# A fused gated-attention and quantised-MLP kernel: the first three steps of its software pipeline written out by themselves

## What is computed

```python
v    = ctx @ Wkv[:, 1024:]
x    = x + tanh(g_xattn) * (v @ Wout + bout)
h    = layernorm(x) * ln1_g + ln1_b          # over 256
h    = bitlinear(h, w1, b1)                  # 256 -> 1024
h    = gelu(h)
h    = layernorm(h) * ln2_g + ln2_b          # over 1024
h    = bitlinear(h, w2, b2)                  # 1024 -> 256
out  = x + tanh(g_ffn) * h
# bitlinear: each row of the input rounded to 127 steps of its largest
# magnitude, the weights to -1, 0, 1 of their mean magnitude
```

## Time and profile before

| | |
|---|---|
| three runs | 412.28, 412.6 and 414.04 us, median 412.6 |
| the profiled execution | 411.33 us, its span 409.5 us |
| busy in the span | DVE 327.3 us (80%), PE 309.5 (76%), ACT 277.6 (68%), POOL 221.4 (54%) |
| mean granted clock of PE | 0.946 |

### The profile page before, as it was taken

How to read it: one execution, slowest core, us unless ns; L and a number is a source line. 1 busy time by engine, 2 the same in 40 slices (tenths; PEclk the granted TensorE clock), 3 DMA queues, 4 the chain that set the end, 5 groups by cost and what they waited for, 6 DMA issues and landing times.

```text
span 409.5 us, 5758 instructions
## 1 busy us (share of the span) xinstructions
PE 309.5 (76%) x1658; PEld 186.5 (46%) x1658; DVE 327.3 (80%) x794; ACT 277.6 (68%) x446; POOL 221.4 (54%) x117
## 2 busy tenths in 40 slices
PE   2846777687969697979797969797979684938365
PEld 2744643343636363636363636363636341515043
DVE  0345461998999999999999999999999996968681
ACT  1202237598887878787888888787878776969421
POOL 4000416577566666666666666666666666664600
PEclk9988889998999999999999999999999996969688
DMA  7941223316365555556555555555552526353625
GB/s 225 378 149 47 81 91 108 89 51 115 117 116 169 113 170 112 171 104 182 108 175 107 178 105 179 103 179 104 128 101 81 101 79 88 93 96 86 153 53 154
DMA packets 98557, 51.59 MB, mean 126 GB/s; under 512 B 87407, under 2 KB 89640, under 8 KB 98526
## 3 DMA queue, kind: packets, MB, share of 16 engines
q1 hardware_dynamic: 96608, 51.00, 49.1%
q10 hardware_dynamic: 1918, 0.23, 0.4%
HBM read 21.78 MB, written 8.46 MB: 74 GB/s over the span
## 4 chain that ended last, share of the span: by engine, by line
DVE 41%; PE 30%; issue 12%; POOL 7%; DMA 5%; ACT 3%; DVEq 0%; POOLq 0%; ACTq 0%
DVE y L657 10%; PE bank_f L904 8%; POOL rstd L295 6%; PE slot_c L864 5%; DVE h L616 5%; DVE amax L624 5%; DVE res L707 5%; PE slot_a L890 4%; DVE amax L661 3%; DMA split_vectors<-vec_parts 3%; PE slot_b L890 3%; DVE x L573 2%; DVE parts L559 2%; PE slot_a L887 2%; PE bank_q L794 2%
## 5 line engine op out<-in xcount | busy, mean ns | idle before, releaser
L311 POOL TENSOR_TENSOR y<-u,g_bc 128x1024 f32<-128x1024 f32 x64 | 150.2, 2369 | 28.7 <-DVE parts L559 25.4
L295 POOL TENSOR_TENSOR rstd<-var,half_neg 128x8 f32<-128x8 f32 x18 | 30.3, 1683 | 129.5 <-DVE var L698 86.1
L657 DVE TENSOR_TENSOR y<-y,slot_c 128x1024 f32<-128x1024 f32 x64 | 77.6, 1212 | 5.0 <-PE slot_c L864 5.0
L661 DVE TENSOR_REDUCE amax<-y 128x1 f32<-128x1024 f32 x64 | 78.1, 1220 | 2.2
L441 ACT ACTIVATE junk<-u,usum 128x1024 bf16<-128x1024 f32 x64 | 73.7, 1151 | 1.2
L414 ACT ACTIVATE q<-y,s 128x1024 f16<-128x1024 f32 x64 | 69.8, 1139 | 5.2 <-DVE s L688 5.0
L843 PE MATMUL bank_q<-wvo,ctxT 128*128 128x256 f32 x256 | 69.1, 402 | 0.0
L904 PE MATMUL bank_f<-w2T,q2T 128*128 128x256 f16 x512 | 64.1, 281 | 0.0
L904 PEld LDWEIGHTS bank_f<-w2T,q2T 128*128 128x128 f16 x512 | 51.5, 101 | 14.3 <-issue 0.8
L405 ACT ACTIVATE q<-h,s 128x256 f16<-128x256 f32 x64 | 27.3, 496 | 41.2 <-DVE s L648 41.1
L864 PE MATMUL slot_c<-ln_rows,rows 128*128 128x512 bf16 x128 | 40.9, 402 | 16.9 <-DVE y L657 8.5
(11 more groups left out here) (104 smaller groups left out, 393.1 us busy)
## 6 DMA issues: line engine op xcount, KB each, us to landing
c_in<-in_ctx SPq DMA_DIRECT2D x16, 512.0 KB, 3.3
x_in<-in_x SPq DMA_DIRECT2D x16, 512.0 KB, 4.6
out<-res SPq DMA_DIRECT2D x32, 256.0 KB, 2.4
y<-in_L_ffn_w SPq DMA_DIRECT2D x2, 1024.0 KB, 12.1
u<-in_L_xattn_Wkv SPq DMA_DIRECT2D x1, 1024.0 KB, 7.0
u<-in_L_xattn_Wout SPq DMA_DIRECT2D x1, 1024.0 KB, 10.6
q2T<-q SPq DMA_TRANSPOSE x64, 3.3
g_bc<-in_L_ffn_ln_g SPq DMA_DIRECT2D x1, 512.0 KB, 12.4
```

The source lines that it names most:

```text
L295: nc.gpsimd.tensor_tensor(rstd[:, :, :], var[:, :, :], half_neg[:, :, :], ALU.pow) \
L311: nc.gpsimd.tensor_tensor(y[:, k % 2, t, :], u[:, t, :], g2_bc[:, :], ALU.mult).then_inc(gain2_done, 1)
L657: nc.vector.tensor_tensor(line, line, slot_c[:, :], ALU.add).then_inc(y_done, 1)
L661: nc.vector.tensor_reduce(amax2[:, t:t + 1], y[:, k % 2, t, :], AX.X, ALU.max, apply_absolute_value=True).then_inc(amax2_done, 1)
```

## The change

- The split vectors go to memory in one transfer instead of three. `load_rows` and the load of `bout_rows` move from ACT to SP, which now waits for that transfer before it issues them and everything behind them (x of step 0, w2, the gains, the inputs of step 1). `load_rows` reads one copy of the three parts three times.
- Bodies -3, -2 and -1 are written out by themselves on PE, ACT and DVE; on POOL body(-2) makes the gain product of step 0 in two halves, ahead of the first root.
- `attention_bank` gives half 1 of step 0 the second half of `slot_c` and half 1 of step 1 `bank_f`, so these two do not wait for the residual of half 0.
- The turned context of step 2 is taken by ACT in body(0), behind `quantise_first(0)`; before, it was taken in body(-1).
- In `second_product` the bias comes behind the products of each group (two products of 256 columns) instead of ahead of both groups (one of 512 columns); the wait for `rows` moves with it.
- In the last body ACT rounds all four groups of step 15 and then takes the rows.

```diff
@@ -50 +50 @@
-    parts_dram = nc.dram_tensor("split_vectors", (NPROD, 4 * H), BF16, kind="Internal").ap()
+    parts_dram = nc.dram_tensor("split_vectors", (NPART, 4 * H), BF16, kind="Internal").ap()
@@ -183,0 +184,6 @@
+        def attention_bank(k, h):
+            if h == 1 and k < 2:
+                return slot_c[:, 512:1024] if k == 0 else bank_f[:, :]
+            return bank_q[:, :]
@@ -235,0 +242,13 @@
+            def load_rows(dst, first, kind, n):
+                source = parts_dram[:, first:first + n].unsqueeze(0).to_broadcast([NPART, NPART, n])
+                for a in range(2):
+                    at = ROWS * a + NPROD * kind
+                    col = n * a if dst.shape[1] > n else 0
+                    sp.dma_start(dst[at:at + NPROD, col:col + n], source).then_inc(rows_in, 16)
+            sp.wait_ge(parts_out, 16)
+            sp.wait_ge(rows_zero, 5)
+            sp.dma_start(bout_rows[0:NPART, :], parts_dram[0:NPART, 3 * H:3 * H + D]) \
+                .then_inc(bout_in, 16)
@@ -239,0 +259,2 @@
+            load_rows(ln1_rows[:, :], 3 * H + D, 0, D)
+            load_rows(ln1_rows[:, :], 3 * H + 2 * D, 1, D)
@@ -241,0 +263,4 @@
+            load_rows(b1_rows[:, :, :].rearrange("p a n -> p (a n)"), 0, 4, H)
+            load_rows(ln2_rows[:, :, :].rearrange("p a n -> p (a n)"), H, 2, H)
+            load_rows(ln2_rows[:, :, :].rearrange("p a n -> p (a n)"), 2 * H, 3, H)
+            load_rows(b2_rows[:, :], 3 * H + 3 * D, 5, D)
@@ -317 +342 @@
-                if i == -1:
+                if i == -2:
@@ -318,0 +344,7 @@
+                    for h in range(2):
+                        two = slice(2 * h, 2 * h + 2)
+                        pool.wait_ge(x1_done, h + 1)
+                        op = nc.gpsimd.tensor_tensor(
+                            h1[:, two, :], x1[:, 0, two, :],
+                            g1_bc[:, :].unsqueeze(1).to_broadcast([P, 2, D]), ALU.mult)
+                    op.then_inc(gain1_done, 1)
@@ -324 +356 @@
-                if live(i + 1):
+                if live(i + 1) and i > -1:
@@ -336,8 +367,0 @@
-            def load_rows(dst, first, kind, n):
-                v = dst.shape[1] // n
-                for a in range(2):
-                    at = ROWS * a + NPROD * kind
-                    act.dma_start(dst[at:at + NPROD, n * (a % v):n * (a % v) + n],
-                                  parts_dram[:, first:first + n]).then_inc(rows_in, 16)
@@ -361,4 +385,2 @@
-            for i in range(NPART):
-                act.dma_start(parts_dram[NPART * i:NPART * (i + 1), :]
-                              .rearrange("j (p n) -> j p n", p=P).rearrange("j p n -> p j n"),
-                              vec_parts[:, :, :]).then_inc(parts_out, 16)
+            act.dma_start(parts_dram[:, :].rearrange("j (p n) -> p j n", p=P), vec_parts[:, :, :]) \
+                .then_inc(parts_out, 16)
@@ -377,4 +398,0 @@
-            act.wait_ge(parts_out, 16 * NPART)
-            act.wait_ge(rows_zero, 5)
-            act.dma_start(bout_rows[0:NPART, :], parts_dram[0:NPART, 3 * H:3 * H + D]) \
-                .then_inc(bout_in, 16)
@@ -382,6 +399,0 @@
-            load_rows(ln1_rows[:, :], 3 * H + D, 0, D)
-            load_rows(ln1_rows[:, :], 3 * H + 2 * D, 1, D)
-            load_rows(b1_rows[:, :, :].rearrange("p a n -> p (a n)"), 0, 4, H)
-            load_rows(ln2_rows[:, :, :].rearrange("p a n -> p (a n)"), H, 2, H)
-            load_rows(ln2_rows[:, :, :].rearrange("p a n -> p (a n)"), 2 * H, 3, H)
-            load_rows(b2_rows[:, :], 3 * H + 3 * D, 5, D)
...
@@ -444,0 +458,2 @@
+                if i == -3:
+                    return
@@ -446 +461,11 @@
-                    weight_copies(0, [w1T[:, k, :] for k in range(KD)])
+                    take_context(1, 0)
+                    weight_copy(0, 0)
+                    take_context(1, 1)
+                    return
+                if i == -1:
+                    take_rows()
+                    weight_copy(0, 1)
+                    weight_copy(1, 0)
+                    weight_copy(1, 1)
+                    nc.scalar.activation(table[:, :], half_neg[:, 0, 0:1], ACT.Gelu)
+                    return
@@ -449,0 +475,3 @@
+                if i == 0:
+                    take_context(2, 0)
+                    take_context(2, 1)
@@ -453 +481 @@
-                if -1 <= i <= S + 1:
+                if i <= S:
@@ -458,4 +486,2 @@
-                if i == -1:
-                    weight_copies(1, [w2T[:, 4 * n:4 * n + 4, :].rearrange("p k d -> p (k d)")
-                                      for n in range(2)])
-                    nc.scalar.activation(table[:, :], half_neg[:, 0, 0:1], ACT.Gelu)
+                if i == S + 1:
+                    take_rows()
@@ -575 +601 @@
-                        in0=bank_q[:, :], scalar=tg[:, 0:1],
+                        in0=attention_bank(k, h), scalar=tg[:, 0:1],
@@ -718,0 +745,26 @@
+                    return
+                if i == -2:
+                    residual(0, 0)
+                    statistics(0, 0)
+                    residual(0, 1)
+                    statistics(0, 1)
+                    for n in range(4):
+                        join(0, n)
+                    scale_weights(1)
+                    round_weights(1, 0)
+                    return
+                if i == -1:
+                    deviations()
+                    for n in range(5):
+                        split(n)
+                    residual(1, 0)
+                    statistics(1, 0)
+                    round_weights(1, 1)
+                    shift_first(0)
+                    for n in range(5):
+                        first(0, n)
+                    residual(1, 1)
+                    statistics(1, 1)
+                    for n in range(4):
+                        join(1, n)
+                    return
@@ -724,4 +776 @@
-                if i == -2:
-                    scale_weights(1)
-                    round_weights(1, 0)
-                if -1 <= i <= S:
+                if i <= S:
@@ -729 +778 @@
-                if -1 <= i <= S + 1:
+                if i <= S + 1:
@@ -764,2 +812,0 @@
-                if i == -2:
-                    round_weights(1, 1)
...
@@ -836 +885 @@
-                    else:
+                    elif k > 1:
@@ -839 +888 @@
-                        acc = bank_q[:, (t % 2) * D:(t % 2 + 1) * D]
+                        acc = attention_bank(k, h)[:, (t % 2) * D:(t % 2 + 1) * D]
@@ -897 +945,0 @@
-                    wait(pe, rows_copied, k + 4)
@@ -899,2 +946,0 @@
-                    nc.tensor.matmul(bank_f[:, :], rows[:, pair, :], b2_rows[:, :], start=True,
-                                     stop=False)
@@ -901,0 +948 @@
+                        acc = bank_f[:, (t % 2) * D:(t % 2 + 1) * D]
@@ -904,4 +951,6 @@
-                            product = nc.tensor.matmul(bank_f[:, (t % 2) * D:(t % 2 + 1) * D],
-                                                       q2T[:, t, j, :], w2T[:, j, :], start=False,
-                                                       stop=(t % 2 == 1 and j == KH - 1))
-                        product.then_inc(ffn_done, 1)
+                            nc.tensor.matmul(acc, q2T[:, t, j, :], w2T[:, j, :], start=(j == 0),
+                                             stop=False)
+                        wait(pe, rows_copied, k + 4)
+                        nc.tensor.matmul(acc, rows[:, pair, :],
+                                         b2_rows[:, (t % 2) * D:(t % 2 + 1) * D], start=False,
+                                         stop=True).then_inc(ffn_done, 1)
@@ -910,2 +958,0 @@
-                    turn_weights(0, lambda n, j: w1_raw[:, j, n * P:(n + 1) * P])
-                    sum_weights(1)
@@ -914,2 +961,10 @@
-                if live(i + 2):
-                    attention(i + 2, 1)
+                    attention(0, 0)
+                    attention(0, 1)
+                    sum_weights(1)
+                    return
+                if i == -2:
+                    turn_context(1, 0)
+                    turn_weights(0, 0)
+                    turn_context(1, 1)
+                    attention(1, 0)
+                    return
@@ -916,0 +972,2 @@
+                    turn_rows()
+                    turn_weights(0, 1)
@@ -917,0 +975,11 @@
+                    shift_first(0)
+                    pe.wait_ge(wscaled, 2)
+                    attention(1, 1)
+                    turn_weights(1, 0)
+                    turn_weights(1, 1)
+                    turn_context(2, 0)
+                    turn_context(2, 1)
+                    attention(2, 0)
+                    return
+                if live(i + 2):
+                    attention(i + 2, 1)
@@ -950,4 +1017,0 @@
-                if i == -2:
-                    turn_weights(1, lambda n, j: w2_raw[:, j % KD, (4 * n + j // KD) * P:
-                                                        (4 * n + j // KD + 1) * P])
```

(27 more changed lines are left out.)

4 lines of the change are left out of this document (2 added, 2 removed).

## The result

The changed kernel takes **402.73 us** (median of 4 runs, 401.95 to 403.77), the kernel before, run beside it, 412.44 (4 runs, 411.33 to 414.04). The ratio is 0.977, 95% interval 0.9741 to 0.9798: faster by 2.3%, or 9.7 us. The forecast was 403.2.

What follows compares the result with a forecast made beforehand. Middle steps were taken as bound by DVE (19.32 of 20.56 us), the start as held by ACT's wait for the split vectors. 411.33 - 9.4 = 401.9 for a profiled-like execution, median 403.2, range 399.6 to 407.0.

Steps and rivals of the forecast that it cites:

- The copy of `wvo`, the landing: Start: `wvo` copied without waiting, 23.2 to 23.8 us; split vectors landed at 16, so nothing waits for loads.
- The rival's late landing: Start: split transfer lands at 20.2, w2 at 26.4, everything moves by 2.9 us to 406.1; chance 0.15.
- Attention of step 0: Start: each half takes 1.95 us at full clock, the second following at once; 25.75 and 27.7.
- Join and root: Start: residual, statistics and join take 2.70 us to POOL's root at 30.45; the root takes 2.48, to 32.95.
- Rows, then ACT's own queue: Start: rows copied at 35.15; then ACT's weight copies and GELU table, not DVE, set the rounding at 42.4.
- Copy, turn, copy: Start: after 1.71 us of rounding, ACT and PE handle the context of step 2 in 1.98, to 46.15.
- Attention of step 2: Start: PE, mostly idle before, runs mostly at the 1.2 GHz level and takes 3.44 us, to 49.6.
- Residual to rows: Start: residual of step 2 to copied rows takes 3.84 us, to 53.5; the transposing DMA is hidden.
- the middle keeps its length: Middle steps: no work is taken from DVE there, so steps stay at 20.56 us.
- The end and the biases: Second products and last body: worth nothing; bounds 0 to 0.80 us per step and 0 to 2.1 us gained.
- The rival of a broken stream: Every step: split biases break PE's stream, 0.80 us per step, 12.0 in all, giving 415.2; chance 0.05.
- 9.4 less: Start: first product of step 0 begins at 53.5 instead of 62.90 us, the whole predicted gain.

Runs made afterwards that it cites:

- loads_not_held: Changed kernel with SP issuing x of step 0, w2 and the first gain ahead of its wait for the split vectors: 402.42 us.
- steps_only: Changed kernel's order with the memory traffic of before (three transfers, wait and twelve row loads on ACT): 412.26 us, ratio 0.9997.
- transfers_only: Kernel before with the new memory part alone (one transfer, its wait and the row loads on SP), old order of bodies: 404.24 us, ratio 0.9806.
- old_end_and_bias: Changed kernel with the old 512-column bias ahead of both groups and the old order of rows and roundings at the end: 403.38 us.
- start_kept_busy: Changed kernel with 64 extra small PE products, 50 before Wv is there and 14 before the context of step 0: 403.09 us.
- one_transfer_act: Changed kernel with one transfer, but its wait and the row loads on ACT, nothing held on SP: 411.76 us, ratio 0.9983.
- pe_kept_busy: Changed kernel with 38 extra products in PE's pauses, around the turns of context 2 and ending bodies 0 and 1: 399.43 us.
- rounding_first: Changed kernel with ACT taking the context of step 2 before the rounding of step 0, w2 copies and GELU table load after it: 396.77 us.
- all_together: rounding_first with the transposing DMA of step 0 issued ahead of two loads, plus extra PE products at the start and ending bodies 0 and 1: 393.05 us.

## Why the prediction was right, and where it was off

The time (402.73 for 403.2) and the place (`hidden(0)` at 53.39 for 53.5) both came out. By its points:

1. *The copy of `wvo`, the landing.* Right: 22.74, the landing at about 16.0 for 16. The rival's late landing was then made on purpose in loads_not_held, and cost nothing, since there w2 and x were not behind it. So what a late landing does with w2 and x behind it was not measured. In the changed kernel the second sum did wait 0.48 us for w2, too little to matter.
2. *Attention of step 0.* Right: residuals at 25.60 and 27.49 for 25.75 and 27.7.
3. *Join and root.* The root began at 30.52 for 30.45, but took 1.72 us, not 2.48. That term was taken from the only such row of before, where POOL had been idle 35.47 us. In steps_only, behind POOL's half gains, it is 1.72 too; in transfers_only, with 28.21 us of idle before it, 2.48.
4. and 5. *Rows, then ACT's own queue.* Rows copied by 34.43 (34.06 + 0.37) for 35.15: the 0.76 of the root. ACT decided from the w2 copies on, as said: 41.55 for 42.4, the lead of point 3 carried on.
6. *Copy, turn, copy.* From the rounding's start 3.95 us (41.55 to 45.50) for 3.75: the turn took 1.13 us and not 0.66, with the clock already low (43.76 to 44.89 lies in a stretch at 0.50).
7. *Attention of step 2.* Low clock, as chosen: both groups at 1.71, 4.04 us from 45.55 to 49.59 for the 3.44 taken. The row of before had its clock come back in its second group, this one did not.
8. *Residual to rows.* 49.62 to 53.25, 3.63 for 3.84. The transposing DMA, 4.2 us with one load issued just ahead of it, was hidden.

So the 0.1 us at `hidden(0)` is luck in part: a root taken 0.76 too long against an attention taken 0.6 and a copy and turn taken 0.2 too short.

**The step that failed** is "the middle keeps its length". It holds from the shift of step 3 on, but not between the shifts of steps 1 and 3, where this profile lost 1.8 us to PE's clock. The other kernels with that order lost 1.5 to 1.9 (loads_not_held, old_end_and_bias, start_kept_busy, one_transfer_act), and steps_only 0.2, its clock falling only once. The forecast looked at the clock only inside the start. pe_kept_busy shows the cause: with the clock held, both steps shrink. The forecast's sum for an execution like the profiled one was 401.9, and the profiled one took 403.77: nearly all of that 1.9 is this loss. In the medians it does not stand out, since the profile of before was 1.1 below its own median and that of the changed kernel 1.0 above; how much a typical execution gives back, the profiles can't say.

*The end and the biases* at nothing: old_end_and_bias agrees, within its interval. The rival of a broken stream is out: a step is 20.55. The forecast's "9.4 less" hid how the parts combine: the traffic alone brings 8.1, the order alone 0.1, both 9.7, and the 1.5 between 8.1 and 9.7 is within the noise. The hit at 402.73 is thus luck in part too: the median came out 0.5 below the forecast, while the profile shows a loss that it did not count.

## What to carry to other kernels

When a wait goes, walk the engine's queue behind it up to the next thing that everybody needs: here a lead of 16.4 us at the rounding (57.95 to 41.55) was worth 9.5 at the first product, because two copies of the context stood behind the rounding and attention behind them ran at the low clock, and setting the copies ahead of the rounding brought some 7 us more. Count a queue's DMA issues as work of the engine that makes them: twelve on ACT took 8.2 us, as long as the transfer they waited for. And a kernel whose TensorE pauses is not shifted in time as a block: look at the granted clock for a few steps beyond the edit, and try fillers in the pauses.

## What the runs showed of the hardware

- **A small transfer beside large loads.** The same transfer of the split vectors landed after 4.2 to 5.0 us in the ten kernels that hold the loads back, and after 8.5 and 9.0 in the two with them under way (one_transfer_act, loads_not_held).
- **Issue cost by form.** A load of nine rows took 0.34 us to issue when it read nine rows, and 0.68 when it read three rows three times (0.69 on ACT). That doubling makes one_transfer_act's 8.21 us.
- **The transposing DMA** of step 0 took 3.1 or 3.2 us with no load issued in the 2 us before it, 4.2 to 4.4 right behind one of 512 KB in six kernels and 5.1 in a seventh (start_kept_busy), and 5.1 right behind two (rounding_first). That two cost more than one is not shown by this.
- **The clock in a step.** Between the shifts of steps 2 and 3 the granted clock stayed at 1.00 in four profiles and the step took 19.90 or 19.91 us; with a fall to 0.50 on the way it took 20.57 to 21.66.
- **A granted clock of 1.00 before the record's first change did not tell the speed.** In the profile of the changed kernel it reads 1.00 from the start, while turned Wv slots took 1.94 and 1.91 us and the first sixteen products 4.51; the second sixteen took 3.58 in each of these profiles. With earlier products the same slots took 1.09 and 1.04. Only where PE had worked before did the record show the fall to 0.50 (13 to 16 us in start_kept_busy). The first sixteen took 3.62 to 5.87 us in these kernels, and the products at low clock would account for it. That is argued from start_kept_busy and all_together, where record and durations agree, and not shown for the others; fillers up to the landing of the context were not tried.
